# Two 512-column parts of an H layer's block rounded, and their low halves made, by one instruction each

## The reference

```python
h = jax.nn.silu(_tlin(x, w1_w, w1_s)) * _tlin(x, w2_w, w2_s)
h = jax.nn.gelu(_tlin(h, h1_w, h1_s), approximate=False)
h = jax.nn.gelu(_tlin(h, h2_w, h2_s), approximate=False)
return _tlin(h, w3_w, w3_s)
```

## Time and profile before

| what | value |
|---|---|
| median of 3 runs | 759.11 us (759.05 to 759.16) |
| the profiled execution | 760.14 us, its span 758.2 us |
| TensorE busy, of the span | 746.4 us, 98% |
| VectorE, ScalarE, GpSimd busy | 597.3, 431.3, 244.6 us |
| H products (lines 1528, 1529) | 448 matmuls each, from 485.6 us on |
| idle time of TensorE just before line 1528, in all | 2.4 us |
| roundings, line 1146 | 144, mean 627 ns |
| low halves, line 2027 | 144, mean 689 ns, 48.7 us of idle time before them, 48.5 of it ended by the rounding |
| granted clock of TensorE | 1.00 from 456 to 750 us |

### The profile page before, as it was taken

One profiled execution on the slowest core, in us unless ns is written; L12 is line 12 of the kernel. 1 busy time (PEld: TensorE's weight loads), 2 busy tenths in 40 slices (PEclk: granted clock), 3 DMA queues, 4 the chain that ended last, 5 costly groups with the idle time before them and its releaser, 6 DMA issues.

```text
span 758.2 us, 11840 instructions
## 1 busy us (share of the span) xinstructions
PE 746.4 (98%) x3699; PEld 630.9 (83%) x3699; DVE 597.3 (79%) x1308; ACT 431.3 (57%) x843; POOL 244.6 (32%) x278
## 2 busy tenths in 40 slices
PE   8999999999999999999999999999999999999996
PEld 6788888888888888888888888888778988888886
DVE  4789979876698999989866667976976749769566
ACT  5788743344465655546443338456756655566773
POOL 2776243233574755747443231000000200100003
PEclk9999999999999999999999999999999999999998
DMA  7800000002445526362452111044435100373201
GB/s 248 322 2 0 2 1 1 1 1 90 175 153 174 164 81 208 97 208 97 146 214 57 28 61 31 1 167 143 163 128 177 57 1 20 147 222 115 108 1 59
DMA packets 31706, 77.15 MB, mean 102 GB/s; under 512 B 8736, under 2 KB 13472, under 8 KB 27808
## 3 DMA queue, kind: packets, MB, share of 16 engines
q1 hardware_dynamic: 31360, 76.18, 29.8%
q10 hardware_dynamic: 288, 0.26, 0.1%
HBM read 58.08 MB, written 16.78 MB: 99 GB/s over the span
## 4 chain that ended last, share of the span: by engine, by line
PE 88%; DVE 4%; ACT 3%; issue 2%; DMA 1%; POOL 1%; SPq 0%; DVEq 0%; ACTq 0%
PE bank L1378 16%; PE bank L1234 11%; PE bank L1528 10%; PE bank L1529 10%; PE bank L1262 8%; PE bank L1356 8%; PE bank L1361 8%; PE bank L1357 8%; PE bank L1377 6%; PE bank L1381 2%; DVE part_r L2027 1%; ACT hring L1146 1%; PE bank L1535 1%; PE bank L1536 1%; DMA wp_lo_f<-in_wproj 1%
## 5 line engine op out<-in xcount | busy, mean ns | idle before, releaser
L1378 PE MATMUL bank<-wx_both,hx_hi 128*128 128x512 f32 x512 | 191.4, 397 | 0.0
L1528 PE MATMUL bank<-hring,wring 128*128 128x512 f32 x448 | 174.5, 390 | 2.4 <-DVE part_r L2027 1.3
L989 ACT ACTIVATE hx_hi<-bank 128x512 fp32r<-128x512 f32 x128 | 76.4, 597 | 175.3 <-PE bank L1361 174.2
L1529 PE MATMUL bank<-part_r,wring 128*128 128x512 f32 x448 | 174.3, 389 | 0.0
L720 POOL TENSOR_TENSOR x_tok<-right,x_tok 128x256 f32<-128x256 f32 x128 | 94.6, 740 | 172.0 <-ACT right L996 168.7
L2027 DVE TENSOR_TENSOR part_r<-part_f,hring 128x512 fp32r<-128x512 f32 x144 | 95.3, 689 | 48.7 <-ACT hring L1146 48.5
L1800 DVE SCALAR_TENSOR_TENSOR hx_lo<-bank,hx_hi 128x512 fp32r<-128x512 f32 x128 | 87.9, 687 | 51.4 <-ACT hx_hi L989 49.9
L1378 PEld LDWEIGHTS bank<-wx_both,hx_hi 128*128 128x128 f32 x512 | 96.0, 188 | 16.7
L1377 PE MATMUL bank<-wx_both,hx_lo 128*128 128x256 f32 x384 | 108.6, 283 | 0.0
L1528 PEld LDWEIGHTS bank<-hring,wring 128*128 128x128 f32 x448 | 84.1, 188 | 20.7 <-DVE part_r L2027 1.7
L1529 PEld LDWEIGHTS bank<-part_r,wring 128*128 128x128 f32 x448 | 84.1, 188 | 17.4
(11 more groups left out here) (209 smaller groups left out, 1418.0 us busy)
## 6 DMA issues: line engine op xcount, KB each, us to landing
wring<-h_dram SPq DMA_DIRECT2D x28, 1024.0 KB, 4.8
wx_raw<-in_wx SPq DMA_DIRECT2D x16, 512.0 KB, 7.6
raw_quads<-in_wffn SPq DMA_DIRECT2D x16, 512.0 KB, 5.6
h_dram<-sums SPq DMA_DIRECT2D x8, 1024.0 KB, 4.4
h_dram<-raw_quads SPq DMA_DIRECT2D x8, 512.0 KB, 6.6
stage<-in_wffn SPq DMA_DIRECT2D x12, 256.0 KB, 2.7
x_tok<-in_x SPq DMA_DIRECT2D x1, 2048.0 KB, 10.9
h_dram<-raw_quads SPq DMA_DIRECT2D x8, 256.0 KB, 6.8
```

The costliest lines, as they stand in the source:

```text
L1378: mm = pe.matmul(DBANK[j][:, :].rearrange("p (h d) -> p h d", h=2), hx_hi[:, place, c, a], wo_hl[:, :, c], start=(c == 0), stop=(c == XC - 1))
L1528: pe.matmul(into[:, :], w, b_hi[:, k], start=(k == 0 and i in (0, 1, 3)), stop=False, skip_group_check=True)
L1529: mm = pe.matmul(into[:, :], w, b_lo[:, k], start=False, stop=(k == KH - 1), skip_group_check=True)
```

## The change

Both functions now return at once for even k. For odd k they handle the parts k - 1 and k by one instruction of 1024 columns, after the wait that belonged to part k, and raise their semaphore by two. In `low_part` two waits are new: f11's low halves wait until the first sum of part k, which reads f11, is done, and f21's until the fourth sum of part k, which reads f21, is done (for the H layers, not for W3). The loops that call the functions are as before: what stood between the calls for k - 1 and k now stands ahead of the joined instruction. Instructions of these two lines go from 144 to 72 each. TensorE's waits are unchanged.

```diff
             def high(q, i, k):
 
+                if k % 2 == 0:
+                    return
                 layer, name = moving(i)
...
-                act.activation(hring[n % 3][:, k], part[at_[name]][:, k], ACT.Copy).then_inc(s_h_hi, 1)
+                act.activation(hring[n % 3][:, k - 1:k + 1], part[at_[name]][:, k - 1:k + 1], ACT.Copy).then_inc(s_h_hi, 2)
...
                 def low_part(q, i, k):
 
+                    if k % 2 == 0:
+                        return
                     layer, name = moving(i)
                     n = q * (TILES_A_PAIR // KH) + i
                     b = PARTS[layer][name]
                     dve.wait_ge(s_h_hi, n * KH + k + 1)
-                    dve.tensor_tensor(part_r[b][:, k], part[b][:, k], hring[n % 3][:, k].bitcast(F32), ALU.subtract).then_inc(s_h_lo, 1)
+                    if layer < 2 and name == "f11":
+                        dve.wait_ge(s_h_sum, summed(q, layer, "t1", k))
+                    if layer < 2 and name == "f21":
+                        dve.wait_ge(s_h_fourth, fourth_done(q, layer, k))
+                    dve.tensor_tensor(part_r[b][:, k - 1:k + 1], part[b][:, k - 1:k + 1], hring[n % 3][:, k - 1:k + 1].bitcast(F32), ALU.subtract).then_inc(s_h_lo, 2)
```

## The result

The change makes the kernel slower: 761.2 us (median of 11 runs, 760.78 to 761.54), beside 759.71 for the kernel before in the same comparison (11 runs). The ratio is 1.0022, its 95% interval 1.0014 to 1.0030, which is 1.1 to 2.3 us. The forecast was 759.05, no change.

A forecast was written before the change was run, and what follows sets the result against it. TensorE, busy nearly throughout, was taken as the bound, with two breaks worth 2.9 us in the H layers. Terms -0.45 + 0.10 + 0.30 = -0.05 took the median of 759.11 to 759.05 us, range 757.9 to 760.2.

The forecast's parts named there:

- part 1: Chains of t1 and t4: two dearer rounds replace four, 7.79 against 7.82 us; dropping the first low half gains 0.60.
- Prices of a joined instruction: For 1024 columns, by the slope of two sizes: ScalarE's copy 1.06 us, VectorE's subtraction 1.23.
- Rival C: Slower: joining delays what TensorE waits for, a pair being as dear as two instructions; 761.6 us, chance 0.09.
- Rival A: Joined chains are really half as long and both TensorE breaks close: 756.5 us, chance 0.06.
- Part 2: W1 and W2: x_high, x_low and the weight load come 0.43 us later, VectorE's run of low halves 0.70 later.
- rival B: Slack takes up the W1 and W2 delay and the tail's delay: 758.3 us, chance 0.18.
- Part 3: The chain from VectorE's low halves at 489.65 to TensorE's stall at 562.34: TensorE 0.45 us earlier after its restart.
- second break: TensorE's stall at 562.34 inside t1's product, 1.42 us late plus 0.11 restart; forecast to remain, about 1.1 wide.
- Part 4: The rest: 0.10 us lost in the first pair's W3 stage, nothing in the second pair, tail 0.30 later.
- allowance of 0.10 in W3: First pair's W3 stage: products that took single parts must wait for whole pairs; 0.10 us lost, allowed rather than summed.
- rival D: A W3 part or f11's pair (2,3) misses its product by more than counted: 759.8 us, chance 0.07.
- sum of -0.05: Whole kernel: -0.45 up to TensorE's restart, +0.10 in W3, +0.30 in the tail, in us.

The follow-up runs named there:

- e1: The changed kernel with both semaphores raised by one per joined instruction and the counts that wait for them halved: 759.83 us, ratio to before 1.0004.
- e6: Only t1 and t4 joined, raised by one, all other blocks part by part as in the kernel before: 758.15 us, ratio 0.9981.
- e7: The kernel before, single parts, with block sum m put ahead of low half m on VectorE in t1 and t4: 756.4 us, ratio 0.9954.
- e3: The changed kernel, raised by two where joined, with f11 of layer 0 made part by part: 760.57 us, ratio 1.0015.
- e4: The changed kernel with the very last block (f21 of W3, second pair of groups) made part by part: 760.83 us, ratio 1.0017.
- e8: All parts joined, raised by one, with block sums ahead of the low halves in t1 and t4: 757.15 us, ratio 0.9967.
- e2: The kernel before, nothing joined, but both semaphores raised by two per part and all counts doubled: 761.29 us, ratio 1.0026.
- e5: The kernel before, nothing joined, with only the roundings' semaphore raised by two and VectorE's waits for it doubled: 759.39 us, ratio 1.0003.

## Why the prediction was wrong

The step that failed is the hand-over. In part 1 it says of the pair "its low halves 1.06 + 0.03". The 0.03 is from rows in which the low half raises its semaphore by one. The change raises by two, which the diff shows, and I gave that no price. The hand-over took 0.10, and with the raise by two the whole kernel took some 1.4 us more than with a raise by one (e1). By the prediction's own steps:

- **Prices of a joined instruction**: right, 1056 and 1223 ns. Rival C rested on dearer ones and so isn't the cause; that its 761.6 comes near the measured 761.2 is chance. The Trainium skill's rule beside it (Perfetto Trace Analysis, Optimizing Scalar/DVE Operations) fits the condition, yet not the result here: joined but counted by one the time stays (e1), and t1 and t4 joined alone gain 0.19% (e6).
- **Part 1, chains of 7.79 instead of 7.82**: 7.75 without the longer hand-over (e1), 7.90 with it. Rival A, chains of half the length, was rightly doubted; what does halve them is the order (e7).
- **Part 2, the delay of 0.43 and 0.70**: right. The weight load waited 0.63 (forecast 0.64), TensorE's start behind it comes 0.37 late, and the run of low halves starts 33.91 after the FFN's start (489.66) instead of 33.16, 0.75 later. e3 shows that this reaches the end, and e4 that the tail's delay does, so rival B falls.
- **Part 3, k = 3 of the second break 0.34 earlier, 0.45 with its restart**: 0.18 earlier in e1, 0.31 with the restart; after the change 0.87 later, 0.77 with it. So the working was already 0.14 too hopeful without the raise by two: block sum 0 of layer 1 comes 0.68 earlier in e1, not 0.87. Of the 1.05 between the two kernels, three chains make 0.45 (7.90 less 7.75, three times). VectorE's waits for its own sums, counted at 0.15 beyond the usual distance, were about 0.18 in e1 (532.23 to 533.01 with 0.60 usual) and 0.22 after. One of them was far longer:

```profile
532.70 0.68 DVE L2040 TENSOR_TENSOR part_f<-part_f 128x512 f32<-128x512 f32 x1
533.87 1.23 DVE L2035 TENSOR_TENSOR part_r<-part_f,hring 128x1024 fp32r<-128x1024 f32 x1 [0.49 <-DVE part_f L2040]
```

  The sum ends at 533.38, its reader starts 0.49 later; the nine other waits of VectorE for its own sums in this kernel take 0.13. The 0.35 stands at the same place in e3 and e4, not in e1, and not in the second pair. What causes it is open. It may go with the raise by two, since e1 has neither. But the separate waits also put 56 more instructions into VectorE's stream than e1 has, and in the three kernels that show the 0.35 a packet of the instruction queue q14 follows the late start by 0.66 us, while in e1 the next one comes only at 540.42. So the loading of code at that place is a rival. Against it, such a packet comes at 533.73 in the kernel before, without a late start. No run separates the two.
- **Part 4**: the allowance of 0.10 in W3 was too small. Between the second break's restart and the last matmul the change loses 0.58 more (0.77 to 1.35), the new break at 591.17 among it; e1 loses 0.25 (0.31 earlier to 0.06 earlier). So rival D holds in part: the W3 stage misses its products by more than I counted. Its other place, f11's pair (2,3), was counted rightly: 0.4 (538.4 against 538.0), and 0.43 in e1. The tail's 0.30 was right as to the pair (0.29 in e1), and the raise adds 0.07.

So the sum of -0.05 was the sum for a kernel that counts by one. That kernel measured 1.0004, and its trace gives -0.06 on TensorE and +0.29 in the tail, 0.23 in all: the misses of parts 3 and 4 are small beside the range. The step that took the result out of the range is the raise by two, some 1.4 us on the run times (1.0022 less 1.0004).

## What to carry to other kernels

When instructions are joined, halve the counts and raise by one, and price a hand-over by rows in which both sides carry the same waits and raises as the new code. Where two engines take turns, look first at which instruction stands behind a wait that it doesn't need: exchanging two lines gave 3.0 us where halving the instructions gave nothing. A joined instruction paid where it dropped an early piece from a serial chain that TensorE waited for (t1 and t4 in e6; no longer in e8, where the order had shortened the chains), and cost where something else waited behind its first half (x_high, the tail).

## What the runs showed of the hardware

A subtraction of VectorE that waited on a semaphore and raised another by two had its wait as an instruction of the sequencer, and started 0.102 us after the end of what it waited for; raised by one, it kept the wait and started after 0.032. This held for 512 columns (e2 against before and e5) and for 1024 (after against e1). It did not matter by how much the awaited semaphore was raised (e5). The separate wait and the later start always came together; that the one makes the other is inferred. The Trainium skill (Trainium Kernel Development and Optimization, section Key Constraints) says that compute semaphores must increment by 1; here raising by two ran, and cost 0.07 us at each such hand-over, 0.2% of the kernel in all.

ScalarE shows a smaller delay of the same kind. In W3's last block its first rounding waits for TensorE to free a ring buffer. It starts 11.20 us ahead of TensorE's last matmul where it raises by one (before, e1, e4, e6, e7, e8) and 11.15 ahead where it raises by two (after, e2, e3, e5), so 0.05 later.
